# One AdaLN transformer block: where the first down projection and the second transposes of the gated hidden layer stand in the fourth block's order

## The reference, cut to what matters

```python
h = layernorm(x) * (1 + ca) + sa
x = x + ga * attention(h)              # 16 heads of 64, causal, softmax, output projection
h = layernorm(x) * (1 + cb) + sb
# fp4 quantise + dequantise in blocks of 16 on both sides of each linear
gate = fp4_linear(h, w_gate)           # 128 -> 352
y    = fp4_linear(h, w_up)             # 128 -> 352
hid  = silu(gate) * y
x = x + gb * fp4_linear(hid, w_down)   # 352 -> 128
```

## Time and profile before

| what | value |
|---|---|
| median of 3 runs | 1363.34 us (1361.21 to 1366.97) |
| the profiled execution, its own time | 1361.84 us |
| span of its trace | 1359.9 us |
| PE busy, matmuls | 1272.2 us, 94% of the span |
| PE weight loads (PEld) | 1032.7 us, 76% |
| DVE busy | 1102.7 us, 81% |
| ACT busy | 835.7 us, 61% |
| POOL busy | 843.4 us, 62% |

### The profile page before, as it was taken

The page is one execution under the profiler, slowest core; times in us unless marked ns, Lnnn a source line. Parts: engine busy times, 40 slices in busy tenths (PEclk is TensorE's granted clock), DMA queues, the critical chain, the costliest instruction groups (busy, mean ns, idle before and its releaser), DMA issues.

```text
span 1359.9 us, 34237 instructions
## 1 busy us (share of the span) xinstructions
PE 1272.2 (94%) x10194; PEld 1032.7 (76%) x10194; DVE 1102.7 (81%) x2565; ACT 835.7 (61%) x2885; POOL 843.4 (62%) x1582
## 2 busy tenths in 40 slices
PE   5999999999999999999999999999999999999973
PEld 3677887777887777787777787777788777788762
DVE  5678888888888888888888888888888888888775
ACT  3766666666666665666765665756666666666640
POOL 1656566766666666666666656576656676666563
PEclk9999999999999999999999999999999999999995
DMA  3000000000000000000000000000000000000000
GB/s 101 17 19 17 18 14 17 21 21 15 21 10 19 20 21 20 17 10 21 17 21 21 15 10 21 17 21 21 15 15 16 17 21 21 15 21 6 19 19 10
DMA packets 38056, 26.53 MB, mean 20 GB/s; under 512 B 2800, under 2 KB 33392, under 8 KB 38032
## 3 DMA queue, kind: packets, MB, share of 16 engines
q1 hardware_dynamic: 38032, 26.23, 6.7%
HBM read 21.94 MB, written 4.28 MB: 19 GB/s over the span
## 4 chain that ended last, share of the span: by engine, by line
POOL 50%; issue 33%; PE 9%; DVE 3%; ACT 2%; POOLq 2%; DMA 1%; SPq 0%; DVEq 0%; ACTq 0%
POOL probs L437 21%; POOL qy L75 6%; POOL qy L73 5%; POOL probs L435 4%; POOL hq L77 3%; PE ps_m L827 3%; POOL h2a L484 2%; POOL rstd L445 2%; PE ps_s L922 2%; POOL h L488 2%; PE ps_o L949 2%; PE ps_m L806 1%; POOL x_keep L479 1%; POOL x_gb L459 1%; POOL xq L77 1%
## 5 line engine op out<-in xcount | busy, mean ns | idle before, releaser
L563 ACT ACTIVATE probs<-ps_s,neg_max 128x128 f32<-128x128 f32 (+1 forms) x1024 | 425.7, 431 | 393.2 <-PE ps_s L931 393.2
L437 POOL TENSOR_SCALAR probs<-probs,r_den 128x256 f32<-128x256 f32 (+1 forms) x768 | 349.3, 472 | 0.0
L736 DVE TENSOR_REDUCE neg_max<-ps_s 128x4 f32<-128x1024 f32 x256 | 303.8, 1218 | 2.5 <-PE ps_s L922 2.1
L922 PE MATMUL ps_s<-qk 64*128 64x256 f32 x2048 | 260.0, 393 | 1.5 <-ACT probs L563 1.0
L435 POOL TENSOR_TENSOR probs<-probs,r_den 128x128 f32<-128x128 f32 x256 | 102.5, 400 | 238.4 <-DVE r_den L745 232.9
L662 DVE COPY probs_t<-ps_m 128x512 f32<-128x512 f32 x256 | 176.4, 689 | 90.7 <-PE ps_m L806 86.5
L806 PE MATMUL ps_m<-ident,probs 128*128 128x128 f32 x1536 | 230.4, 273 | 1.4 <-DVE probs_t L662 0.8
L922 PEld LDWEIGHTS ps_s<-qk 64*128 64x128 f32 x2048 | 186.1, 187 | 49.1 <-issue 12.4
L563 ACT ACTIVATION_READ_ACCUMULATOR probs<-ps_s,neg_max 128x1 f32 x1024 | 218.6, 213 | 0.0
L949 PE MATMUL ps_o<-probs_t,v 128*64 128x256 f32 (+1 forms) x2048 | 194.7, 332 | 1.6 <-ACT o_t L555 1.6
L73 POOL TENSOR_TENSOR qy<-qy,qm 128x352 f32<-128x352 f32 (+1 forms) x96 | 83.1, 865 | 180.4 <-DVE qm L66 178.6
(11 more groups left out here) (107 smaller groups left out, 1804.1 us busy)
## 6 DMA issues: line engine op xcount, KB each, us to landing
mod_a<-mod_rows SPq DMA_DIRECT2D x32, 256.0 KB, 3.3
x_in<-L_attn_x SPq DMA_DIRECT2D x32, 128.0 KB, 2.1
x_res<-L_attn_x SPq DMA_DIRECT2D x32, 128.0 KB, 2.1
out<-y_out SPq DMA_DIRECT2D x32, 128.0 KB, 1.8
mod_b<-mod_rows SPq DMA_DIRECT2D x32, 64.0 KB, 2.8
wkv<-L_attn_Wkv SPq DMA_DIRECT2D x2, 512.0 KB, 6.9
wq<-L_attn_Wq SPq DMA_DIRECT2D x1, 512.0 KB, 4.0
wo<-L_attn_Wo SPq DMA_DIRECT2D x1, 512.0 KB, 8.1
```

What stands on the lines that cost most here:

```text
L437: ins = nc.gpsimd.tensor_scalar(cols, cols, r_den[:, u % 4, s:s + 1], 1.0, ALU.mult, ALU.mult)
L563: ins = nc.scalar.activation(probs[:, u % 4, h, t * P:(1 + 2 * t) * P], ps_s[:, 2 * (u % 2) + h, t * N:t * N + (1 + t) * P], ACT.Exp, bias ...
L736: nc.vector.tensor_reduce(neg_max[:, u % 4, :], ps_s[:, 2 * (u % 2):2 * (u % 2) + 2, :].rearrange("p b (t j) -> p (b t) j", t=2), AX.X, AL ...
L922: mm = nc.tensor.matmul(ps_s[:, 2 * (u % 2) + h, t * N:(t + 1) * N], qk[rows, u % 4, 0, t * P:(t + 1) * P], qk[rows, u % 4, 1, :], start=( ...
```

## The change

In the fourth tuple of `SHARED`, place 3 held `hqt` 1 and now holds `down` 0. Place 4 holds `t2` in both. Place 5 held `qk1` and now holds `hqt` 1; place 6 held `down` 0 and now holds `qk1`. Place 7 keeps `down` 1. `down` k on PE now waits for the copy of its own half of `hq_t`, where both used to wait for both copies.

```diff
-            ("t0", "qk0", "t1", ("hqt", 2, 1), "t2", "qk1", ("down", 2, 0), ("down", 2, 1)))
+            ("t0", "qk0", "t1", ("down", 2, 0), "t2", ("hqt", 2, 1), "qk1", ("down", 2, 1)))
...
                 elif kind == "down":
-                    pe.wait_ge(hqt_ready, 2 * (b + 1))
+                    pe.wait_ge(hqt_ready, 2 * b + k + 1)
```

## The result

The changed kernel takes 1324.3 us (median of 4 runs, 1322.91 to 1326.48), beside 1362.67 for the kernel before. The ratio is 0.9715, 95% interval 0.9688 to 0.9742, so 2.85% faster; the two medians differ by 38.4 us. The sign was right, and the gain that I forecast, 19.8 us, was half of what came. The time is nearest to rival A (1329).

What follows compares the result with a forecast made beforehand. PE was taken to set the 40.48 us period, waiting 1.21 us for POOL's L77. 30 x 0.58 + 2.4 = 19.8 us off 1361.84 gives 1342.0, with 1.5 more for the median 1343.5; range 1328 to 1354.

Steps and rivals of the forecast that it cites:

- rival A: On DVE, unit 7's denominators not held by L75: PE keeps 1.06 us per iteration, 34.2 us, 1329; chance 0.22.
- PE up to hqt 1: On PE before `hqt` 1: `down` 0 (0.87 us) and `t2` fill the 1.21 us wait for L77, leaving some 0.05.
- PE behind it: On PE after `hqt` 1: the next iteration's scores begin at 620.57 instead of 621.63, 1.06 us gained per iteration.
- DVE: On DVE before the first mask: unit 7's denominators wait for L75's end; new 0.5 us PE wait leaves 0.58 us.
- E: End of L66, in the quantisation of `h2`: 0.71 us later than before, at 621.36.
- rival B: On DVE, `y_out` held by L75, then denominators by L77; period as before, only the end won: 1361 to 1363; chance 0.08.
- the caught case: Unit 7's denominators on DVE wait until POOL's L75 ends: 0.58 us gained per iteration, 1343.5 us; chance 0.58.
- ACT: ACT idles 1.44 us at its copy of `hqt` 1, holding back `exponentials(7, 0)` and the copy of `t2`.
- The end: Last two iterations, without probabilities: `down` 0 runs in PE's wait for L77, 1.23 us each, 2.4 us in all.
- C: Three banks for eight steps: PE would wait at `qk1` for `down` 0's bank, read late by DVE; 1361; chance 0.06.
- D: On DVE, reading `down` 0 delays unit 6's denominators beyond 0.71 us; up to 0.5 us lost per iteration, 1376; chance 0.06.

Runs made afterwards that it cites:

- Experiments 2 and 3: Kernel before, with only `t2` (2) or only `down` 0 (3) moved ahead of `hqt` 1: 1343.26 us and 1331.99 us.
- Experiment 6: Changed kernel with one, three or ten tiny DVE memsets ahead of the denominators of unit 7, which L75 then held: 1335.92, 1336.46, 1335.74 us.
- Experiment 5: Changed kernel, but ACT reads places 4 and 5 (`t2`, `hqt` 1) ahead of `exponentials(7, 0)`: 1333.48 us, beside 1325.38 for the changed kernel run again.
- experiment 4: Changed kernel with `hqt` 1 one place further back, behind `qk1`: 1374.81 us, ratio 1.0097 to the kernel before.

## Why the prediction fell short, by its own steps

**PE up to hqt 1: right.** The 1.21 us hole was filled and L77's end did not move. `down` 0 took 0.67 us there (601.32 to 601.99) and not the 0.87 that I took from the one in front of the scores. So PE came earlier to `hqt` 1 and still has a gap of 0.28 us in its weight loads instead of 0.05; as L77 sets that moment either way, that costs nothing of the forecast. Experiments 2 and 3 show the two parts: 0.75 and 0.52 us of wait remain when only one of them is moved.

**PE behind it: too small by 0.17.** I had 1.06 us, and it is 1.23. The small error above came back here: with `t2` done 0.2 us sooner, ACT copied it and `hqt` 1 sooner (to 603.81, that is 1.07 us after `hqt` 1 began, where I had 1.30), and `down` 1 started 1.18 us after `hqt` 1 instead of 1.35. This term alone, 30 x 0.17 = 5 us, took the time out of my range: rival A's 1329 was inside it.

**DVE: the step that failed.** I let the denominators of unit 7 be caught by L75 and priced that at 0.5 us of PE's time before the mask. They were not caught, and the wait of PE that took 0.48 us out of my 1.06 did not come. I said that both instructions hang on E, 0.96 and 0.90 us behind it, and let these 0.06 us decide. One term put me on the wrong side. I added a gap of 0.16 us between `y_out` and the denominators, because it stood there before, and it did not come again: they begin 0.07 us before `y_out`'s recorded end. Against that, `y_out` was held by L73 and took 0.59 instead of 0.29 us, which I had left out. Why the gap stood there before, no run shows. In the end the denominators began 0.88 us after L66's end, where I had 0.96, and L75 0.89 after it, where I had 0.90. By the rows, the hold that I left out sets the order: both instructions follow the end of L73, at 0.07 and 0.08 us, in 29 of 30 iterations. So it was not the near toss that 0.58 against 0.22 made of it. I had used such a hold of `y_out` in rival B alone, for `down` 1 beside L75. Experiment 6 prices the step on its own: 11 to 12 us. That a caught instruction waits for the end of POOL's was right, and so was the place where it would cost.

**E, the moment of L66's end: 0.18 too late.** The denominators of unit 6 did take 0.16 us instead of 0.43, as forecast. But they began 0.63 us after `ffn`, not 0.68, and `ffn` itself came earlier with the shorter `down` 0. The shift was 0.53 us (3.73 less 3.20 from L77's begin) instead of 0.71. With this alone the caught case gains 0.76 and not 0.58 per iteration, 1338; the experiment with the catch has 1336.

**ACT: right in direction, not priced.** I named the wait of ACT for `hqt` 1 and then only used ACT's times. Experiment 5 shows that 8 us of the gain need it.

**The end: too large.** From the second half's L77 of the last iteration with attention to the end of the trace it was 54.47 us (from 1305.48) and is 52.53 (from 1268.72). That is 1.9 us for my thirtieth iteration and my 2.4 us together. The last iteration alone gave 1.3 us, about the 1.23 that I took the earlier trace rows; the two steps from L77 to L77 ahead of it gave 0.24 and 0.40, so something else than the down projection sets L77 there. What it is, is not shown.

**The rivals.** A was what happened, at 1329 priced 5 us short by the 0.17 above. C did not come: the repeated gap vanished while the three banks stayed, so the rule of the Trainium skill that I had weighed (Perfetto Trace Analysis, Optimization Strategy) does not fit this gap; its releaser, POOL's L77, had said so. B and D did not come. D's price of 0.5 us does not follow from its terms either: L65 and L66 doubled are 0.8 us. A loss against the kernel before exists one place further, in experiment 4, but by ACT's order and the clock and not by D's holds.

No version run here beats the changed kernel; at 39.11 busy of 39.25 us, PE leaves 0.14 us per iteration, some 4 us in all, to a better order.

## What to carry to other kernels

When an engine waits at the same spot in every iteration, look for work of its own behind the wait that is ready ahead of it, and count what stands between the end of the wait and the next dependence: the period shrinks by what leaves that stretch, and the reader engines' lists must follow (one place too far cost 50 us here, 42 by the order and 8 by the clock). Where a forecast hangs on which of two instructions starts first, by less than 0.1 us, look first for what releases each of them, as here the end of one and the same POOL instruction; if that does not settle it, give the two outcomes like chances and let the range reach to both. A duration read in front of one kind of successor is not the one in front of another: a down projection took PE 0.67 us ahead of transposes and 0.87 ahead of the scores.

## What the runs showed of the hardware

A DVE instruction of 0.17 us lasts 0.67, 0.61 or 0.42 when it begins 0.08, 0.15 or 0.33 us behind a POOL tensor_tensor of 0.73, always ending 0.02 to 0.03 us after it, and 0.17 when it begins 0.01 us ahead (the 0.61 is the run with three memsets). The Trainium skill (SBUF — State Buffer, Who interferes with whom) says of a DVE instruction in a mode that uses both pairs of ports: who issues first gets the pair that both engines share for its whole instruction, and the other is blocked. For the DVE instruction that comes second the trace agrees; which mode it runs in, no view shows. For POOL coming second the trace shows little: L75 behind the denominators took 0.75 us instead of 0.73, though they lasted for another 0.16. One memset of 0.06 us was enough to swap the order, and cost 0.9% of the kernel. The list of waits does not name such a hold, since it stands in the instruction's own duration.

A DVE tensor_tensor with both inputs in SBUF was held too: `y_out` beside L73 took 0.59 instead of 0.29 and ended at 606.52, 0.15 us after L73 (606.37). The next DVE instruction then began 0.07 to 0.08 us behind L73's end and POOL's next one 0.08, in 29 of 30 iterations.
